# A spiking feed-forward block: the idle row's products move from TensorE to ScalarE and GpSimd, and x comes in 16 loads

## The chip, the core and the metric

The kernel runs on one core of one Trainium2 chip. The core has five engines that run their own instruction streams and meet only at semaphores: TensorE (PE, matrix products; weight loads are shown as PEld), VectorE (DVE), ScalarE (ACT), GpSimd (POOL) and SyncE (SP, which only issues transfers here). Transfers run on 16 DMA engines. The metric is the device time of one execution in microseconds. Before the change it is 115.94 us, the median of three runs (115.93 to 116.21).

## The reference

`x` is (2, 2048, 512). An integrate-and-fire stage turns it into spikes, and a two-layer network is applied to them and added to `x`:

```python
rates = relu(x) * 0.001
c = cond[:, None, :] + cumsum(rates, axis=1)
fl = floor(c)
spikes = (fl - shift(fl)) / 0.001            # mostly 0; a spike is 1000
h = relu(einsum('bsd,dw->bsw', spikes, w1) + b1)      # w1: 512 x 2048
out = x + einsum('bsw,wd->bsd', h, w2) + b2           # w2: 2048 x 512
```

In most tokens no feature spikes. There the network gives the same row for all: the "idle row", `relu(b1) @ w2 + b2`. Over a sequence each of the 2 x 512 features crosses its threshold about once, so at most 1024 of the 4096 rows differ from `x` plus the idle row.

## The kernel before

**What it computes.** Tokens are laid out 16 to a partition: partition p of `x_sb[b]` holds tokens 16p to 16p+15 of sequence b. Five streams of work stand beside each other.

1. *The table* (PE, L718). For a token in which exactly one feature d spikes, the row to be added is a fixed function of d. The kernel computes that row for all 512 features: for each of 16 chunks m of the hidden layer, ScalarE turns the chunk of w1 into `relu(1000*w1 + b1) - relu(b1)` (L380, L381), and PE multiplies it with the chunk of w2 into four PSUM tiles `ps_table` (four products 128x512 in float32 a chunk; the trace shows each as two MATMUL records). The weights of a chunk come as one 512 KB transfer ("pair").
2. *The search* (DVE, with small PE products). `block_totals` adds up relu(x) over the 16 tokens of a partition (L475, L477); `turn_totals` transposes the sums on PE (L749); `block_sums` and `find_blocks` make running sums and find the block in which each feature crosses its threshold; GpSimd gathers those 16 values by indirect DMA (L319, `rates`); `find_tokens` finds the token; PE spreads the tokens (`spread_tokens`, L759), DVE counts which tokens meet others (`count_met`, L537), `find_leads` and `count_leads` number the shared ones, and `find_slots` puts them in 128 slots. All this is done for b = 0 and for b = 1; b = 1 ends later.
3. *The idle row* (PE). `add_strips` multiplies `relu_b1` with w2 in 16 products of 32 output partitions each (L731); ScalarE copies the four strips, `join_strips` adds them with one 128x512 product (L739), ScalarE copies again into `idle_base`, and DVE adds b2 (`finish_idle_row`).
4. *The stores*. `add_idle` (L613) adds the idle row to 4 tokens a partition, 2.2 us for 1 MB; SP stores each of the eight pieces (L280) as soon as it is there. When a sequence's four stores have landed, GpSimd adds table rows into the output by indirect DMA (`add_row`, L324), four scatters for each sequence. These are the single-spike tokens.
5. *The general rows*. For tokens with more spikes, `first_spikes` and `second_spikes` build the spike columns, PE runs both layers (L788, 128 products of 128x128 with ScalarE's relu L399 behind them, then L795, 16 products 128x512), DVE subtracts the idle base (L649) and GpSimd scatters one last time (L324, `to_general`). At the end GpSimd waits for all scatters, loads a flag (`redo_count`, a register load from SBUF) and skips a branch that does not run with these inputs.

**What sets the order.** Each engine's stream is written out by hand. On PE the table's chunks are the filler into which the small products of the search are set at fixed places; an instruction there that has to wait stops all behind it. The same holds for DVE and GpSimd. SP issues the loads in the order in which they are written, alternating a pair and 1 MB of x, and all the loads share the DMA engines.

## Time and profile before

| | |
|---|---|
| median of 3 runs | 115.94 us (115.93 to 116.21) |
| the profiled execution | 116.06 us |
| its span, first to last instruction | 114.2 us |
| PE busy | 97.1 us (85%), 370 instructions |
| DVE busy | 72.2 us (63%) |
| ACT busy | 33.8 us (30%) |
| POOL busy | 27.0 us (24%) |
| DMA | 31.40 MB, mean 275 GB/s |

The profiled execution took 1.86 us more than its span; that part lies outside the instructions. A busy share says how long an engine had work, not that it set the time: an engine can be at 85% and still have room at the place that matters. Views in the section of rows are named by what they show. In a timeline row the columns are start, duration (us), engine, line, operation, output<-input, shape and count, and in brackets the idle time ahead and what ended it.

### The profile page before, as it was taken

The numbers are of one execution on the slowest core, as the hardware profiler recorded it, in microseconds if no ns is written. First come the engines' busy times: TensorE is split into PE (matmuls) and PEld (weight loads), VectorE is DVE, ScalarE is ACT, GpSimd is POOL, SyncE is SP. The second block draws the span as 40 slices with busy tenths as digits, with TensorE's granted clock in tenths as the row PEclk, the third lists the DMA queues.
The fourth block names the chain that finished last, engine by engine and source line by source line (L and its number), as shares of the span: only waits on it lengthen the run. The fifth ranks groups of instructions, "written<-read, shape, count | busy, mean of one in ns | idle before, by whom it ended". The sixth has DMA issues, their size and how long they took to land. (4 is left out here: it accounts for less than half of the span.)

```text
span 114.2 us, 1132 instructions
## 1 busy us (share of the span) xinstructions
PE 97.1 (85%) x370; PEld 51.2 (45%) x370; DVE 72.2 (63%) x161; ACT 33.8 (30%) x59; POOL 27.0 (24%) x32
## 2 busy tenths in 40 slices
PE   0079999999999989999969999999999999996000
PEld 0043444445433444243424754459999944441000
DVE  2004899678999999889778759999999200002000
ACT  3445542354235189930102000006834400000000
POOL 6600000000037400074000000000048740578500
PEclk9999999999999999999999999999999999999975
DMA  1999999999999999999700000699879999477730
GB/s 39 263 368 419 417 429 425 416 417 416 423 413 404 395 390 408 386 384 380 267 13 0 0 0 6 275 413 413 367 324 413 316 327 278 78 77 96 88 47 3
DMA packets 9002, 31.40 MB, mean 275 GB/s; under 512 B 1570, under 2 KB 1698, under 8 KB 7072
## 3 DMA queue, kind: packets, MB, share of 16 engines
q1 hardware_dynamic: 7152, 29.37, 65.5%
q0 software_dynamic: 1552, 1.64, 10.3%
q10 hardware_dynamic: 288, 0.27, 0.9%
q8 instruction: 5, 0.08, 0.4%
q14 instruction: 5, 0.04, 0.1%
HBM read 21.31 MB, written 10.75 MB: 281 GB/s over the span
## 5 line engine op out<-in xcount | busy, mean ns | idle before, releaser
L718 PE MATMUL ps_table<-w_sb 128*128 128x512 f32 x128 | 59.5, 615 | 6.3 <-DMA w_sb<-in_w_pairs 6.3
L718 PEld LDWEIGHTS ps_table<-w_sb 128*128 128x128 f32 x128 | 24.4, 197 | 36.0 <-issue 29.7
L477 DVE SCALAR_TENSOR_TENSOR total<-x_sb,total 128x512 f32<-128x512 f32 x30 | 20.7, 691 | 3.2 <-DMA x_sb<-in_x 2.3
L324 POOL DMA_INDIRECT out<-w_sb,to_single x8 | 13.4, 1674 | 39.2 <-DMA out<-x_sb 37.4
L380 ACT ACTIVATE w_sb<-w_sb,b_col 128x512 f32<-128x512 f32 (+1 forms) x17 | 11.8, 691 | 22.5 <-DMA w_sb<-in_w_pairs 22.5
L319 POOL DMA_INDIRECT rates<-in_x_turned,sixteen_at x8 | 8.4, 1049 | 39.9 <-DVE sixteen_at L503 38.1
L613 DVE TENSOR_TENSOR x_sb<-x_sb,idle_row 128x2048 f32<-128x2048 f32 x8 | 17.8, 2282 | 0.0
L795 PE MATMUL ps_idle<-w_sb 128*128 128x512 f32 x32 | 13.9, 592 | 0.0
L381 ACT ACTIVATE w_sb<-w_sb,minus_relu_b 128x512 f32<-128x512 f32 (+1 forms) x17 | 11.8, 697 | 0.6
L649 DVE TENSOR_TENSOR w_sb<-ps_idle,idle_base 128x512 f32<-128x512 f32 x1 | 0.7, 692 | 15.6 <-PE ps_idle L795 15.6
L795 PEld LDWEIGHTS ps_idle<-w_sb 128*128 128x128 f32 x32 | 6.0, 190 | 7.2 <-issue 7.2
L399 ACT ACTIVATE w_sb<-ps_turn,b_col 128x128 f32<-128x128 f32 x8 | 2.9, 368 | 19.2 <-PE ps_turn L788 19.2
L788 PE MATMUL ps_small<-spk_t,w_sb 128*128 128x128 f32 x64 | 8.5, 275 | 0.0
L788 PE MATMUL ps_turn<-spk_t,w_sb 128*128 128x128 f32 x64 | 8.5, 275 | 0.0
L788 PEld LDWEIGHTS ps_turn<-spk_t,w_sb 128*128 128x128 f32 x64 | 7.9, 192 | 0.5 <-issue 0.5
L788 PEld LDWEIGHTS ps_small<-spk_t,w_sb 128*128 128x128 f32 x64 | 7.8, 192 | 0.0
L475 DVE TENSOR_SCALAR total<-x_sb 128x512 f32<-128x512 f32 x2 | 0.9, 427 | 7.2 <-DMA x_sb<-in_x 7.2
L731 PE MATMUL ps_idle<-w_sb,relu_b 128*32 128x512 f32 x32 | 4.1, 601 | 0.0
L399 ACT ACTIVATE w_sb<-ps_small,b_col 128x128 f32<-128x128 f32 x8 | 2.9, 368 | 3.2 <-PE ps_small L788 3.1
L537 DVE SCALAR_TENSOR_TENSOR same<-ps_turn,token,weigh 128x512 bf16<-128x512 f32 x4 | 3.0, 751 | 0.3 <-DVE hot L556 0.2
L537 DVE SCALAR_TENSOR_TENSOR same<-ps_met,token,weigh 128x512 bf16<-128x512 f32 x4 | 3.0, 750 | 0.1
L749 PEld LDWEIGHTS ps_turn<-ident_dt,total 128*128 128x128 f32 x16 | 1.9, 191 | 2.0 <-DVE total L477 2.0
(111 smaller groups left out, 52.6 us busy)
## 6 DMA issues: line engine op xcount, KB each, us to landing
out<-x_sb SPq DMA_DIRECT2D x8, 1024.0 KB, 4.4
w_sb<-in_w_pairs SPq DMA_DIRECT2D x15, 512.0 KB, 20.1
x_sb<-in_x SPq DMA_DIRECT2D x7, 1024.0 KB, 18.4
w_sb<-in_w SPq DMA_DIRECT2D x4, 1024.0 KB, 18.3
x_sb<-in_x SPq DMA_DIRECT2D x2, 512.0 KB, 6.8
w_sb<-in_w_pairs SPq DMA_DIRECT2D x2, 256.0 KB, 4.1
b_row<-in_b ACTq DMA_DIRECT2D x1, 256.0 KB, 4.3
rates<-in_x_turned,sixteen_at POOLq DMA_INDIRECT x8, 5.4
```

What stands on the lines that cost most here:

```text
L319: pool.indirect_dma_start(out=rates[:, col, :], out_offset=None, in_=x_sixteen, in_offset=bass.IndirectOffsetOnAxis(ap=sixteen_at[:, col:c ...
L324: pool.indirect_dma_start(out=out_rows, out_offset=bass.IndirectOffsetOnAxis(ap=to, axis=0), in_=row, in_offset=None, bounds_check=last_ro ...
L380: chain(act.activation(weights, weights, ACT.Relu, bias=b1_col[:, m:m + 1], scale=PER_DT))
L381: act.activation(weights, weights, ACT.Identity, bias=minus_relu_b1[:, m:m + 1]).then_inc(table_hidden_ready, 1)
L399: act.activation(hidden[m], ps_hidden[m % 2][:, 0:P], ACT.Relu, bias=b1_col[:, m:m + 1], scale=PER_DT).then_inc(ready, 1)
L477: last = dve.scalar_tensor_tensor(out=total[b][:, :], in0=x_sb[b][:, t, :], scalar=0.0, in1=total[b][:, :], op0=ALU.max, op1=ALU.add)
L537: chain(dve.scalar_tensor_tensor(out=same[:, :], in0=ps_spread[b][:, :], scalar=token[:, col:col + 1], in1=weigh[:, (3 - c) * P:(7 - c) * ...
L613: dve.tensor_tensor(tokens, tokens, along(idle_row[:, :], TQ), ALU.add).then_inc(idle_added[b][q], 1)
L718: last = pe.matmul(ps_table[c][:, :], table_hidden[:, m, c * P:(c + 1) * P], w2_sb[:, m, :], start=(m == 0), stop=(m == FC - 1))
L731: last = pe.matmul(ps_idle[strip, :], relu_b1[:, m:m + 1].to_broadcast([P, STRIP]), w2_sb[:, m, :], start=(m < STRIPS), stop=(m >= FC - ST ...
L788: last = pe.matmul(ps_hidden[m % 2][:, 0:P], w1_sb[:, c, m * P:(m + 1) * P], spk_t[:, c, :], start=(c == 0), stop=(c == DC - 1))
L795: last = pe.matmul(ps_out[:, :], hidden[m], w2_sb[:, m, :], start=(m == 0), stop=(m == FC - 1))
```

## The change

Six things are changed together.

- `add_strips` and `join_strips` are gone from PE. ScalarE multiplies each chunk of w2 with `relu_b1` as a per-partition scale (`scale_second`, 16 activations 128x512, into four buffers `scaled`), GpSimd adds the sixteen up (`sum_idle`, 15 additions 128x512, each waiting for the one ahead), and PE sums over the partitions with one product by a matrix of ones (`add_idle_parts`). One of ScalarE's two copies from PSUM goes as well. GpSimd's additions are set around its gathers: 1 to 6 ahead of those of b = 0, 7 to 10 ahead of those of b = 1, and 11 to 15 behind these.
- x comes in 16 loads of 512 KB instead of one pair of half loads and seven of 1 MB; each pair of weights now stands 512 KB earlier in SP's order. `b1_col` and w2's first chunk are issued by ScalarE's queue.
- ScalarE prepares chunk 0 in four pieces and chunk 1 in two.
- PE's small products stand at other places among the table's.
- On DVE `rise_levels` and `names` come first; `find_odd` goes behind `find_leads(0)`; the first `add_idle` goes ahead of `second_spikes`; `list_general` goes behind the last `add_idle`.
- GpSimd loads the redo flag ahead of the last scatter, and waits for the scatters to land at the very end.

```diff
-            for b in range(B):
-                for q in range(XQ):
-                    if b > 0 or q > 0:
-                        load_x(b, q)
-                        load_pair(b * XQ + q + 2)
-            for m in range(B * XQ + 2, FC):
+            load_x(1)
+            load_x(2)
+            for m in range(3, FC):
                 load_pair(m)
+                for h in (2 * m - 3, 2 * m - 2):
+                    if h < B * XH:
+                        load_x(h)
...
+            def sum_idle(begin, end):
+                for m in range(begin, end):
+                    pool.wait_ge(scaled_ready, m + 1)
+                    before = scaled[0] if m == 1 else idle_part
+                    last = pool.tensor_tensor(idle_part[:, :], before[:, :], scaled[m % 4][:, :], ALU.add)
+                    if m < FC - 1:
+                        chain(last)
+                        pool.sem_inc(scaled_used, 1)
+                    else:
+                        last.then_inc(idle_part_ready, 1)
...
+            def scale_second(m):
+                act.wait_ge(w_in[m] if m > 0 else w2_first_in, 16)
+                if m >= 4:
+                    act.wait_ge(scaled_used, max(m - 4, 1))
+                act.activation(scaled[m % 4][:, :], w2_sb[:, m, :], ACT.Copy, scale=relu_b1[:, m:m + 1]).then_inc(
+                    scaled_ready, 1)
...
-            act.wait_ge(strips_summed, 1)
-            act.activation(idle_base[:, :], ps_idle[:, :], ACT.Copy).then_inc(strips_copied, 1)
...
+            def add_idle_parts():
+                pe.wait_ge(idle_part_ready, 1)
+                pe.wait_ge(const_ready, 3)
+                pe.matmul(ps_idle[:, :], ones[:, :], idle_part[:, :], start=True, stop=True).then_inc(idle_summed, 1)
...
+            pool.wait_ge(redo_ready, 1)
+            redo = redo_count(pool)
             pool.wait_ge(general_listed, 1)
             pool.wait_ge(row_ready, 1)
             add_row(to_general[:, :], new_row, general_scattered)
-            pool.wait_ge(singles_scattered, 16 * NE)
-            pool.wait_ge(general_scattered, 16)
...
+            pool.wait_ge(singles_scattered, 16 * NE)
+            pool.wait_ge(general_scattered, 16)
```

The next two listings show PE's stream from `turn_totals(0)` (`ps_turn<-ident_dt,total`) to `spread_tokens(0)` (`ps_met<-ident,token`); `ps_table` are the table's products, `ps_idle` the strips. Before:

```order
L749 MATMUL ps_turn<-ident_dt,total 128x128 x4
L718 MATMUL ps_table<-w_sb 128x512 x9
L731 MATMUL ps_idle<-w_sb,relu_b 32x512 x4
L718 MATMUL ps_table<-w_sb 128x512 x7
L749 MATMUL ps_turn<-ident_dt,total 128x128 x4
L718 MATMUL ps_table<-w_sb 128x512 x5
L731 MATMUL ps_idle<-w_sb,relu_b 32x512 x4
L718 MATMUL ps_table<-w_sb 128x512 x4
L759 MATMUL ps_met<-ident,token 128x128 x4
```

And after (its first row is the 23 table products ahead of the first turn; before there were 19):

```order
L743 MATMUL ps_table<-w_sb 128x512 x23
L763 MATMUL ps_turn<-ident_dt,total 128x128 x4
L743 MATMUL ps_table<-w_sb 128x512 x18
L763 MATMUL ps_turn<-ident_dt,total 128x128 x4
L743 MATMUL ps_table<-w_sb 128x512 x8
L773 MATMUL ps_met<-ident,token 128x128 x4
```

The turn of b = 1 stands behind 41 table products instead of 35, and no strips stand between.

On GpSimd, from the last constant on (`rates` are the gathers, `idle_part` the additions, `to_single` and `to_general` the scatters), it is this after the change:

```order
L307 AFFINE_SELECT weigh<-weigh 128x896
L316 TENSOR_TENSOR idle_part<-scaled 128x512
L316 TENSOR_TENSOR idle_part<-idle_part,scaled 128x512 x5
L328 DMA rates<-in_x_turned,sixteen_at 128x16 x4
L316 TENSOR_TENSOR idle_part<-idle_part,scaled 128x512 x4
L328 DMA rates<-in_x_turned,sixteen_at 128x16 x4
L316 TENSOR_TENSOR idle_part<-idle_part,scaled 128x512 x5
L335 DMA out<-w_sb,to_single 4096x512 x8
L246 TENSOR_LOAD redo_i
L246 ISA x2
L335 DMA out<-w_sb,to_general 4096x512
```

Before, only the eight gathers and the nine scatters stood there, and the TENSOR_LOAD behind the last of them.

On DVE, from the idle row on (`x_sb<-x_sb,idle_row` is `add_idle`, `spk_t<-ps_met,token,spk_t` is `second_spikes`, `single` begins `list_singles`), it is this after the change:

```order
L627 TENSOR_TENSOR idle_row<-b_row,idle_base 128x512
L587 TENSOR_TENSOR spk_t<-token,ps_met 128x512
L573 SCALAR_TENSOR_TENSOR slot<-leads_run,ps_small,leads 128x4
L575 TENSOR_TENSOR hot<-slot,slot_name 128x512
L578 COPY check_sums<-ps_small 128x2
L632 TENSOR_TENSOR x_sb<-x_sb,idle_row 128x2048
L592 SCALAR_TENSOR_TENSOR spk_t<-ps_met,token,spk_t 128x128 x4
L632 TENSOR_TENSOR x_sb<-x_sb,idle_row 128x2048 x3
L581 TENSOR_TENSOR single<-is_first,leads 128x8
L582 TENSOR_SCALAR not_single<-single 128x8
L583 TENSOR_TENSOR to_single<-token,not_single 128x8
L632 TENSOR_TENSOR x_sb<-x_sb,idle_row 128x2048 x4
```

Before, `second_spikes` stood ahead of the first four additions, and eleven more small instructions of `list_general` stood between the two groups of four.

## Rows read from the trace of the kernel before

**Rows 1.** Timeline of GpSimd: gathers, scatters; in brackets idle time and its end.
```profile
3.17 0.28 POOL L305 TENSOR_SCALAR_AFFINE_SELECT upper<-ones 128x128 f32<-128x128 f32 x1
...
48.33 0.95 POOL L319 DMA_INDIRECT rates<-in_x_turned,sixteen_at  x1 [9.63 <-DVE sixteen_at L503]
...
52.10 0.95 POOL L319 DMA_INDIRECT rates<-in_x_turned,sixteen_at  x1 [0.30 <-issue]
84.45 1.90 POOL L324 DMA_INDIRECT out<-w_sb,to_single  x1 [31.39 <-DMA out<-x_sb]
...
98.52 1.55 POOL L324 DMA_INDIRECT out<-w_sb,to_single  x1 [5.98 <-DMA out<-x_sb]
...
104.09 1.55 POOL L324 DMA_INDIRECT out<-w_sb,to_single  x1 [0.30 <-issue]
106.27 1.55 POOL L324 DMA_INDIRECT out<-w_sb,to_general  x1 [0.62 <-issue]
```

**Rows 2.** DMA issues: count, KB each, median us from issue to landing.
```profile
out<-x_sb SPq DMA_DIRECT2D x8, 1024.0 KB, 4.4
...
out<-w_sb,to_general POOLq DMA_INDIRECT x1, 4.8
```

**Rows 3.** Timeline of VectorE, from the second spikes to the end.
```profile
68.28 1.12 DVE L573 SCALAR_TENSOR_TENSOR spk_t<-ps_met,token,spk_t 128x128 f32<-128x128 f32 x4 [1.08 <-PE ps_met L779]
69.32 8.88 DVE L613 TENSOR_TENSOR x_sb<-x_sb,idle_row 128x2048 f32<-128x2048 f32 x4
...
80.36 8.88 DVE L613 TENSOR_TENSOR x_sb<-x_sb,idle_row 128x2048 f32<-128x2048 f32 x4
104.81 0.69 DVE L649 TENSOR_TENSOR w_sb<-ps_idle,idle_base 128x512 f32<-128x512 f32 x1 [15.57 <-PE ps_idle L795]
```

**Rows 4.** Stretches of 2 us: engines' busy time, clock, DMA share, GB/s.
```profile
74.00:76.00 2.00, 2.00 (x6) 0.95 (x5) 2.00 (x2) 0.00 (x0) 0.00 (x0) 1.00 1.02 422
...
82.00:84.00 2.00, 2.00 (x20) 2.00 (x20) 2.00 (x2) 0.91 (x4) 0.00 (x0) 1.00 0.52 217
...
92.00:94.00 2.00, 2.00 (x6) 0.87 (x5) 0.00 (x0) 0.00 (x0) 0.54 (x1) 1.00 1.04 299
```

**Rows 5.** Timeline of TensorE; a table product is two records.
```profile
6.34 18.76 PE L718 MATMUL ps_table<-w_sb 128*128 128x512 f32 x38 [6.34 <-DMA w_sb<-in_w_pairs]
...
26.07 7.89 PE L718 MATMUL ps_table<-w_sb 128*128 128x512 f32 x18
33.90 1.07 PE L731 MATMUL ps_idle<-w_sb,relu_b 128*32 128x512 f32 x8
34.89 6.28 PE L718 MATMUL ps_table<-w_sb 128*128 128x512 f32 x14
41.55 1.16 PE L749 MATMUL ps_turn<-ident_dt,total 128*128 128x128 f32 x8 [0.39 <-DVE total L477]
42.55 4.46 PE L718 MATMUL ps_table<-w_sb 128*128 128x512 f32 x10
...
52.00 1.92 PE L731 MATMUL ps_idle<-w_sb,relu_b 128*32 128x512 f32 x16
...
59.01 0.65 PE L759 MATMUL ps_turn<-ident,token 128*128 128x128 f32 x4 [0.96 <-DVEq L529]
...
76.59 1.05 PE L788 MATMUL ps_turn<-spk_t,w_sb 128*128 128x128 f32 x8
```

**Rows 6.** Timeline of ScalarE, table chunks 0 and 9.
```profile
5.08 0.51 ACT L380 ACTIVATE w_sb<-w_sb,b_col 128x256 f32<-128x256 f32 x1 [1.60 <-DMA w_sb<-in_w_pairs]
...
39.50 0.72 ACT L380 ACTIVATE w_sb<-w_sb,b_col 128x512 f32<-128x512 f32 x1 [3.35 <-DMA w_sb<-in_w_pairs]
```

**Rows 7.** Timeline of VectorE: sums of b = 1 and its search.
```profile
32.82 8.68 DVE L477 SCALAR_TENSOR_TENSOR total<-x_sb,total 128x512 f32<-128x512 f32 x12
...
43.67 1.22 DVE L486 TENSOR_TENSOR_SCAN level<-block_keep,ps_turn 128x512 f32<-128x512 bf16 x1
...
57.41 0.19 DVE L521 TENSOR_SCALAR rates<-rates 128x64 f32<-128x64 f32 x1 [0.82 <-DMA rates<-in_x_turned,sixteen_at]
```

More of the change, by code:

```diff
@@ L71, in spike_ffn @@
         idle_base = sb("idle_base", [P, D])
+        idle_part = sb("idle_part", [P, D])
+        scaled = [sb(f"scaled{i}", [P, D]) for i in range(4)]
         idle_row = sb("idle_row", [P, D])
@@ L387, in _ @@
             act.wait_ge(b1_ready, 2)
-            table_chunk(0, slice(0, 2 * P))
-            table_chunk(0, slice(2 * P, D))
-            for m in range(1, FC):
+            def scale_second(m):
[4 more added lines that the diff above has]
+                    scaled_ready, 1)
+            for c in range(DC):
+                table_chunk(0, slice(c * P, (c + 1) * P))
+            for half in range(2):
+                table_chunk(1, slice(half * 2 * P, (half + 1) * 2 * P))
+            scale_second(0)
+            for m in range(2, FC):
                 table_chunk(m, slice(0, D))
-            act.wait_ge(strips_summed, 1)
-            act.activation(idle_base[:, :], ps_idle[:, :], ACT.Copy).then_inc(strips_copied, 1)
+                scale_second(m - 1)
+            scale_second(FC - 1)
             act.wait_ge(idle_summed, 1)
@@ L640, in _ @@
             find_slots(1)
+            add_idle(0, 0)
             second_spikes()
-            for q in range(XQ):
+            for q in range(1, XQ):
                 add_idle(0, q)
             list_singles()
-            list_general()
             for q in range(XQ):
                 add_idle(1, q)
+            list_general()
             dve.wait_ge(out_summed, 1)
@@ L712, in _, with parts_ready @@
         def _(pe):
+            def parts_ready(m, end):
+                if m == 0:
+                    return end
+                return DC + (end + 1) // 2 if m == 1 else DC + m + 1
             def table_part(m, begin, end):
-                pe.wait_ge(table_hidden_ready, m + 2 if end > 2 or m > 0 else 1)
+                pe.wait_ge(table_hidden_ready, parts_ready(m, end))
                 if m == 0:
@@ L724, in table_chunk @@
                 table_part(m, 0, DC)
-            def add_strips(begin, end):
-                pe.wait_ge(b1_ready, 1)
-                for m in range(begin, end):
-                    pe.wait_ge(w_in[m] if m > 0 else w2_first_in, 16)
-                    strip = slice(m % STRIPS * STRIP, (m % STRIPS + 1) * STRIP)
-                    last = pe.matmul(ps_idle[strip, :], relu_b1[:, m:m + 1].to_broadcast([P, STRIP]), w2_sb[:, m, :],
-                                     start=(m < STRIPS), stop=(m >= FC - STRIPS))
-                if end == FC:
-                    last.then_inc(strips_summed, 1)
-            def join_strips():
-                pe.wait_ge(strips_copied, 1)
-                pe.wait_ge(strip_first_ready, 1)
-                pe.matmul(ps_idle[:, :], strip_first[:, 0:1].to_broadcast([P, P]), idle_base[:, :],
-                          start=True, stop=True).then_inc(idle_summed, 1)
+            def add_idle_parts():
+                pe.wait_ge(idle_part_ready, 1)
+                pe.wait_ge(const_ready, 3)
+                pe.matmul(ps_idle[:, :], ones[:, :], idle_part[:, :], start=True, stop=True).then_inc(idle_summed, 1)
             def turn_totals(b):
```

96 lines of the change are left out of this document (43 added, 53 removed).

## The prediction

> **What bounds the kernel now.** The page gives PE 85% and everything else far less, so the first thing to ask is whether PE sets the end. I read the end of the trace first, then went backwards engine by engine. The last instruction that shows is GpSimd's scatter of the general rows, from 106.27 [rows 1]; it lands 4.8 us later [rows 2], at 111.07, and the span ends at 114.2. Two chains meet in front of it. One is PE's: the second layer ends and DVE's subtraction runs from 104.81 to 105.50 [rows 3]. The other is GpSimd's own: the four scatters of sequence 1 run from 98.52 to 104.09 + 1.55 = 105.64 [rows 1]. They end 0.14 us apart. So a faster PE alone brings nothing; the scatters stand right beside it.
>
> What started the scatters? The row at 98.52 names the landing of the stores. SP stores a piece when DVE has added the idle row; the first addition starts at 69.32, four take 8.88 us (2.22 each), and the second four start at 80.36, 2.16 us behind the end of the first four [rows 3]. While stores run, the DMA engines are full (share 1.02 at 422 GB/s), but in 82 to 84 the share falls to 0.52 [rows 4]: the four stores of sequence 0 are through and the fifth, added at 80.36 to 82.58, is only starting. From 84.45 on GpSimd's scatters share the DMA engines, and the share stays full at 299 GB/s [rows 1, 4]. So the store chain is: first addition, 8 MB through full DMA engines with one hole of about 0.9 us, four scatters, last scatter. The 26.98 us from the first addition's end (71.54) to 98.52 are transfer time, not DVE time.
>
> In front of the first addition stands the search of sequence 1. DVE's sums end at 41.50, `find_bases(0)` fills DVE to 43.67, the running sums start there [rows 7], and from there DVE's chain runs nearly without holes to 67.20 (68.28 less the wait of 1.08 [rows 3]); its one wait on the way is for the gather, 0.82 us at 57.41 [rows 7]. PE serves this chain from between table products.
>
> **The change part by part.**
>
> *PE's strips and join.* The strips cost 0.99 us for four (33.90 to the next start at 34.89) [rows 5], so 16 of them some 3.9 us; the join is a product of the size of the new `add_idle_parts`, so they cancel. PE is 3.9 us shorter. What that buys depends on the two chains above.
>
> *PE's start.* The first transfer has one fewer ahead of it and the first piece is 128 columns instead of 256 (0.51 us each for two activations [rows 6]); I take 0.65 us together, so PE starts at 5.7 instead of 6.34. Each pair comes 512 KB earlier, some 1.25 us at 420 GB/s; chunk 9 before arrives at 39.50 [rows 6] and now near 38. PE wants it at about 39.5 behind ScalarE's 1.4 us: just in time, a wait of 0 to 0.4.
>
> *The turn of sequence 1.* This is the step against the change. PE's first 19 products take at most 18.76 us, a product at speed costs (33.90 - 26.07) / 9 = 0.87, a turn 1.0 (41.55 to 42.55) [rows 5]. After: 5.7 + 18.7 gives 24.4 at most, 4 x 0.87 gives 27.9, the turn 28.9, and 18 x 0.87 gives 44.5; where the first 19 go quicker, since they no longer end in a wait, it is 43.7. I take 44.0. Its result can be read 1.16 later [rows 5], at 45.2, where DVE began at 43.67 [rows 7]. So the search of sequence 1 starts 1.5 us later. The turn of sequence 0 comes at 27.9 instead of 25.08; DVE then is still in the first sums of sequence 1, which the smaller loads of x leave where they are, and it costs nothing.
>
> From 45.2 on everything shifts by 1.5: the gather on GpSimd from 48.33 to 49.8, the wait that ends at 57.41 to 58.9. `find_odd`, moved behind `find_leads(0)`, only fills that wait. DVE reaches the point of 67.20 at 68.7.
>
> *The first addition.* It no longer waits for the slots (1.08 us) nor stands behind the spikes (1.12 us, start to start 1.04) [rows 3]. It begins at 68.7 instead of 69.32 and ends at 70.9 instead of 71.54: 0.6 us earlier. A transfer of 1 MB takes 2.5 us at 422 GB/s [rows 4]; the second addition ends at 70.9 + 1.1 + 2.2 = 74.2, so the DMA engines idle about 0.7 us there, and sequence 0 is through near 82.4, where it was about 82.3. But `list_general` has gone from between the two groups: the fifth addition ends at 74.2 + 4.4 + 0.5 + 2.2 = 81.3 instead of 82.58, and the hole of rows 4 closes. Sequence 1 starts moving at 82.4 instead of about 83.3, and lands 0.9 us earlier, 97.6.
>
> *The end.* Four scatters take 7.12 (98.52 to 105.64) [rows 1], so they end at 104.7. PE meanwhile starts the first layer behind `second_spikes`, at 70.9 + 1.1 = 72.0 instead of 76.59, 4.6 us earlier [rows 5], and DVE's last subtraction ends at 100.9. It is hidden with 3.8 us to spare. The last scatter no longer waits for it and needs 0.3 of idle instead of 0.62 [rows 1]: another 0.3. Loading the flag moves from behind the landing to in front of the scatter. It stands on the same chain in both places, so I count 0; no row shows its duration, but the 3.1 us between landing (111.07) and the end hold it, so it costs between -1 us, if GpSimd does it while the scatter ahead is still being worked on, and 0.5 if it is slower beside them.
>
> *ScalarE.* 16 more activations of 0.72 us [rows 6]. Up to chunk 9 the chunks come 3.8 us apart and three activations need 2.1. Later ScalarE falls to 2.1 us a chunk, and PE needs 3.5. Hidden; chunk 15 is ready about 53, and PE begins it near 64.
>
> *GpSimd's additions.* No row of before shows one. From below: DVE does a two-input 128x512 in 0.69 [rows 3]. The nearest row is GpSimd's own 128x128 select with one input, 0.28 [rows 1], for 512 columns 1.12; with two inputs read one after the other 2.24. I take 1.1 plus 0.06 between two. The Trainium skill ("GPSIMD Engine Reference", section on elementwise cycle accounting) has 4497 ns for 2048 columns, which as an estimate is 1.12 us here; nothing above rests on it. Additions 11 to 15 begin when the gathers end (52.10 + 0.95 + 1.5 = 54.6) and end at 54.6 + 5 x 1.16 = 60.4. PE wants the sum behind the spread of sequence 1, at 59.01 + 0.6 [rows 5] + 1.5 = 61.1. Covered by 0.7 us. Past 1.3 us an addition it would be late by five times the excess.
>
> *Sum.* -0.9 (stores) - 0.3 (last wait) = -1.2 us of the profiled execution's 116.06, 114.86. The median of the runs is 0.12 lower, so I predict 114.7. If the turn comes at 43.7 or 44.5 this is 0.3 less or 0.5 more.
>
> **The rivals.**
>
> *A: GpSimd's additions hold up DVE.* DVE's sums read two tiles (`x_sb`, `total`), as GpSimd's additions do. In before no GpSimd instruction with an input runs beside DVE: the selects are over at 4.7 us and the gathers are the only thing there (DVE's 12 sums beside four of them take 8.68 / 12 = 0.72, their usual price [rows 7]). So nothing in the trace excludes that one waits for the other. Where each addition stops DVE for its 1.16: additions 7 to 9 fall in the sums of sequence 1, which end at 41.50 + 3.5 = 45.0 instead; `find_bases(0)` takes 2.17 and addition 10 falls in it, 48.3. That is 3.1 us behind the 45.2 above, and all that follows shifts: 114.7 + 3.1 = 117.8. It decides from the point where DVE's sums end later than 43.0, since up to there PE's turn at 44.0 and `find_bases(0)` hide it: two additions in full are hardly hidden.
> The Trainium skill says just this ("SBUF - State Buffer", section "Who interferes with whom"): a VectorE instruction with two SBUF inputs and a GpSimd instruction that reads SBUF share a read port, and the second to start waits for the first to finish. No row here shows it. By that rule the time would be the rival's.
>
> *B: the additions are slow.* At 2.3 us each the last five end at 66.1, 5.0 us after PE wants them, and the slots of both sequences stand behind `add_idle_parts` on PE: 119.7. Nothing speaks for it but the missing row.
>
> *C: it cancels.* One addition's worth of delay, or a chunk that PE waits a microsecond for, takes back the 1.2: 115.9. The stores move the same 8 MB through the same full engines, and the margins above are tenths.
>
> *D: PE does count.* If sequence 1 were stored sooner than I think, by the 3.8 us, the end would be PE's, 111. The full DMA share against it makes this 1 in 100.
>
> **How the numbers follow.** The forecast 0.52 (own range 113.6 to 115.5), A 0.26, B 0.07, C 0.14, D 0.01. A measurement tells 0.3%, some 0.35 us, from no change. Faster: the forecast and D and a little of C, 0.54; same 0.13; slower A and B, 0.33. The range goes from the forecast with the flag's load hidden to A's price, 113.5 to 118.0.
>
> **What would show it.** Right: the first `add_idle` near 68.7, the fifth ending near 81.3, no half-empty slice between, the scatters of sequence 1 from 97.6, PE's first layer at 72.0 with its end 4 us ahead of the last scatter. The running sums of sequence 1 on DVE at 45.2, with PE's turn just ahead; where DVE's sums end after 43 and single rows of L496 take over 1 us, it is A; where PE waits for `idle_part`, it is B. Wrong altogether, if the scatters start later than 98.5.

## The result and the profile after

| | before | after |
|---|---|---|
| median of the runs | 115.94 us (115.83 to 116.21) | 118.72 us (117.23 to 119.97) |
| ratio, 95% interval | | 1.012 (1.0084 to 1.0156) |
| profiled execution, its span | 116.06, 114.2 | 117.51, 115.7 |
| forecast, range | | 114.7, 113.5 to 118.0 |

The change makes the kernel slower by 1.2%, some 1.4 us, and by 2.8 us if the two medians of the table are compared. Two of the four executions of after came near 120 us, at granted clocks no lower than those of the others (0.977 and 0.966 against 0.973 and 0.969), and the ratios here and below leave out executions more than 1.5% above the fastest of their kernel, so that for after 117.2 and the profiled 117.5 remain. The forecast was wrong in sign. What came is the mechanism of rival A, GpSimd's additions holding up DVE.

The page's engine shares say at once which way the work went:

```profile
PE 93.0 (80%) x338; PEld 50.5 (44%) x338; DVE 83.4 (72%) x159; ACT 44.4 (38%) x80; POOL 49.6 (43%) x47
```

PE is down as planned. DVE is up, though the change gives it no new work. Its group of the sums over x, in the page's list of the costliest groups, has as many instructions of the same shape as before, where they were 20.7 us at 691 ns each; the second line is what the view of that source line answers in the same trace (ns of the shortest, the median, the longest):

```profile
L496 DVE SCALAR_TENSOR_TENSOR total<-x_sb,total 128x512 f32<-128x512 f32 x30 | 27.7, 923 | 1.0
...
L496 DVE SCALAR_TENSOR_TENSOR total<-x_sb,total x30: 686/693/1919, 11.6 to 43.9; 128x512 f32<-128x512 f32 x30
```

The median is unchanged, and the mean has grown by 232 ns: a few instructions take up to 1919 ns, most of the others their usual 693. A slower engine or tile would lift the median; a long tail under an unchanged median points to somebody in the way. The timelines say who. First DVE's, at the places that answer to [rows 3, 7]:

```profile
33.69 11.81 DVE L496 SCALAR_TENSOR_TENSOR total<-x_sb,total 128x512 f32<-128x512 f32 x12
45.43 1.24 DVE L527 TENSOR_SCALAR some<-blocks_under 128x4 f32<-128x4 f32 x1
...
48.75 1.22 DVE L505 TENSOR_TENSOR_SCAN level<-block_keep,ps_turn 128x512 f32<-128x512 bf16 x1
...
61.10 1.21 DVE L567 TENSOR_TENSOR_SCAN leads_run<-ones,leads 128x4 f32<-128x4 f32 x1
62.55 1.24 DVE L603 TENSOR_SCALAR under_zero<-start_c 128x8 f32<-128x8 f32 x1
64.22 1.03 DVE L540 TENSOR_SCALAR rates<-rates 128x64 f32<-128x64 f32 x1
...
74.88 2.29 DVE L632 TENSOR_TENSOR x_sb<-x_sb,idle_row 128x2048 f32<-128x2048 f32 x1
```

And GpSimd's in the same execution, which answers to [rows 1]:

```profile
40.30 1.28 POOL L316 TENSOR_TENSOR idle_part<-idle_part,scaled 128x512 f32<-128x512 f32 x1
41.77 1.51 POOL L316 TENSOR_TENSOR idle_part<-idle_part,scaled 128x512 f32<-128x512 f32 x1 [0.18 <-POOL idle_part L316]
43.45 1.50 POOL L316 TENSOR_TENSOR idle_part<-idle_part,scaled 128x512 f32<-128x512 f32 x1 [0.18 <-POOL idle_part L316]
45.14 1.50 POOL L316 TENSOR_TENSOR idle_part<-idle_part,scaled 128x512 f32<-128x512 f32 x1 [0.18 <-POOL idle_part L316]
...
61.03 1.26 POOL L316 TENSOR_TENSOR idle_part<-idle_part,scaled 128x512 f32<-128x512 f32 x1 [0.18 <-POOL idle_part L316]
62.47 1.29 POOL L316 TENSOR_TENSOR idle_part<-idle_part,scaled 128x512 f32<-128x512 f32 x1 [0.18 <-POOL idle_part L316]
63.94 1.26 POOL L316 TENSOR_TENSOR idle_part<-idle_part,scaled 128x512 f32<-128x512 f32 x1 [0.18 <-POOL idle_part L316]
...
91.98 3.62 POOL L335 DMA_INDIRECT out<-w_sb,to_single  x1 [26.78 <-DMA out<-x_sb]
...
101.51 1.55 POOL L335 DMA_INDIRECT out<-w_sb,to_single  x1 [0.30 <-issue]
...
108.94 1.55 POOL L335 DMA_INDIRECT out<-w_sb,to_general  x1 [0.30 <-issue]
```

Lay the ends side by side. DVE's `some` ends at 46.67, the addition from 45.14 at 46.64. `leads_run` ends at 62.31 and its addition at 62.29; `under_zero` at 63.79 and its addition at 63.76; `rates` at 65.25 and its addition at 65.20. Four small DVE instructions, 4 to 64 elements wide, which take 0.16 to 0.21 us when nothing runs beside them, each end 0.02 to 0.05 us behind a GpSimd addition. Note that the profile shows this nowhere as a wait: no bracket stands on these DVE rows, since no semaphore is involved. It is hidden in the durations. So the engines do not meet only at semaphores, as the section on the chip puts it.

The account from before to after, by the starts of rows on the way to the end:

| row | before | after | shift | a new part |
|---|---|---|---|---|
| running sums of sequence 1 | 43.67 | 48.75 | +5.08 | +5.08 |
| first `add_idle` | 69.32 | 74.88 | +5.56 | +0.48 |
| fifth scatter | 98.52 | 101.51 | +2.99 | -2.57 |
| last scatter | 106.27 | 108.94 | +2.67 | -0.32 |
| span's end | 114.2 | 115.7 | +1.5 | -1.17 |

So 5.6 us were lost ahead of the first addition of the idle row, and 4.1 were gained behind it. The experiments take both halves apart. Here and below, the running sums are the scan L486 (L505 in after), and the sums are the additions of x ahead of it.

### The profile page after: what moved, and what is told of

Same layout as the page of the kernel before. It is cut to its first block, busy times and chain, and to the rows that moved or that the text cites. A ratio compares the mean times of both kernels' runs of the same rounds, so it can differ in the third digit from the quotient of the medians.

```text
span 115.7 us, 1143 instructions
## 1 busy us (share of the span) xinstructions
PE 93.0 (80%) x338; PEld 50.5 (44%) x338; DVE 83.4 (72%) x159; ACT 44.4 (38%) x80; POOL 49.6 (43%) x47
## 4 chain that ended last, share of the span: by engine, by line
DVE 45%; PE 20%; POOL 10%; issue 9%; DMA 5%; ACT 3%; ACTq 2%; POOLq 0%; DVEq 0%
PE ps_table L743 19%; DVE total L496 10%; POOL out L335 10%; DVE x_sb L632 8%; DMA out<-x_sb 5%; DVE same L556 5%; DVE level L505 2%; DVE under L528 1%; DVE under L519 1%; DVE block_sum L510 1%; DVE hot L575 1%; DVE blocks_under L520 1%; DVE sum_at L531 1%; DVE leads_run L567 1%; DVE some L527 1%
## 5 line engine op out<-in xcount | busy, mean ns | idle before, releaser
L743 PE MATMUL ps_table<-w_sb 128*128 128x512 f32 x128 | 58.8, 612 | 6.0 <-ACT w_sb L395 6.0
L743 PEld LDWEIGHTS ps_table<-w_sb 128*128 128x128 f32 x128 | 24.5, 197 | 34.1 <-issue 26.6
L496 DVE SCALAR_TENSOR_TENSOR total<-x_sb,total 128x512 f32<-128x512 f32 x30 | 27.7, 923 | 1.0
L335 POOL DMA_INDIRECT out<-w_sb,to_single x8 | 14.5, 1815 | 28.9 <-DMA out<-x_sb 26.8
L316 POOL TENSOR_TENSOR idle_part<-idle_part,scaled 128x512 f32<-128x512 f32 x14 | 19.6, 1399 | 13.3 <-ACT scaled L407 12.0
L394 ACT ACTIVATE w_sb<-w_sb,b_col 128x512 f32<-128x512 f32 (+2 forms) x20 | 12.6, 629 | 14.0 <-DMA w_sb<-in_w_pairs 13.9
L407 ACT ACTIVATE scaled<-w_sb,relu_b 128x512 f32<-128x512 f32 x16 | 11.3, 707 | 6.9 <-POOLq L319 6.9
L395 ACT ACTIVATE w_sb<-w_sb,minus_relu_b 128x512 f32<-128x512 f32 (+2 forms) x20 | 12.7, 636 | 0.7
L316 POOL TENSOR_TENSOR idle_part<-scaled 128x512 f32<-128x512 f32 x1 | 1.6, 1621 | 7.8 <-ACT scaled L407 7.8
L420 ACT ACTIVATE idle_base<-ps_idle 128x512 f32<-128x512 f32 x1 | 0.6, 597 | 7.9 <-PE ps_idle L754 7.9
```

What stands on the lines that cost most here:

```text
L316: last = pool.tensor_tensor(idle_part[:, :], before[:, :], scaled[m % 4][:, :], ALU.add)
L335: pool.indirect_dma_start(out=out_rows, out_offset=bass.IndirectOffsetOnAxis(ap=to, axis=0), in_=row, in_offset=None, bounds_check=last_ro ...
L394: chain(act.activation(weights, weights, ACT.Relu, bias=b1_col[:, m:m + 1], scale=PER_DT))
L395: act.activation(weights, weights, ACT.Identity, bias=minus_relu_b1[:, m:m + 1]).then_inc(table_hidden_ready, 1)
L407: act.activation(scaled[m % 4][:, :], w2_sb[:, m, :], ACT.Copy, scale=relu_b1[:, m:m + 1]).then_inc(scaled_ready, 1)
L496: last = dve.scalar_tensor_tensor(out=total[b][:, :], in0=x_sb[b][:, t, :], scalar=0.0, in1=total[b][:, :], op0=ALU.max, op1=ALU.add)
```

## The experiments

Each batch ran beside the kernel before on its own chip, at 116.08, 116.02 and 115.84 us; ratios are to these.

**What the additions cost in all.** `a_noadds` is the changed kernel without additions 1 to 14, so that its idle row lacks most of its terms.

```diff
                     pool.wait_ge(scaled_ready, m + 1)
-                    before = scaled[0] if m == 1 else idle_part
-                    last = pool.tensor_tensor(idle_part[:, :], before[:, :], scaled[m % 4][:, :], ALU.add)
                     if m < FC - 1:
-                        chain(last)
                         pool.sem_inc(scaled_used, 1)
                     else:
-                        last.then_inc(idle_part_ready, 1)
+                        pool.tensor_tensor(idle_part[:, :], scaled[(m - 1) % 4][:, :], scaled[m % 4][:, :],
+                                           ALU.add).then_inc(idle_part_ready, 1)
```

> The changed kernel with GpSimd's additions 1 to 14 left out (waits and counts stay; the idle row is then wrong). Theory 1, the additions hold up VectorE: the 12 sums of sequence 1 take 8.7 us again instead of 11.8, the first add_idle begins near 69 instead of 74.9, and the time falls to about 113.5 to 114.5. Rival, the delay comes from the transposed place of PE's turn or from the smaller loads: the sums still take over 10 us or the first add_idle stays past 72, time over 116.5.

Measured: 111.27 us (111.19 to 111.57), ratio 0.959 (0.955 to 0.963), span 109.4, 2.2 us below the least that I had expected. DVE's timeline:

```profile
33.42 8.68 DVE L494 SCALAR_TENSOR_TENSOR total<-x_sb,total 128x512 f32<-128x512 f32 x12
...
45.58 1.22 DVE L503 TENSOR_TENSOR_SCAN level<-block_keep,ps_turn 128x512 f32<-128x512 bf16 x1 [1.35 <-PE ps_turn L761]
...
68.68 2.29 DVE L630 TENSOR_TENSOR x_sb<-x_sb,idle_row 128x2048 f32<-128x2048 f32 x1
```

The sums are back at 8.68 us. The running sums wait for PE's turn (45.58; the prediction had 45.2), the first addition starts at 68.68 (68.7), and PE's first layer at 72.06 (72.0). Fourteen GpSimd instructions, for whose end nobody stands waiting in after, cost 6.2 us, and without them this kernel is 4.8 us faster than before. GpSimd's timeline of the end:

```profile
85.86 3.54 POOL L333 DMA_INDIRECT out<-w_sb,to_single  x1 [29.59 <-DMA out<-x_sb]
...
95.27 1.54 POOL L333 DMA_INDIRECT out<-w_sb,to_single  x1 [0.30 <-issue]
...
102.66 1.54 POOL L333 DMA_INDIRECT out<-w_sb,to_general  x1 [0.30 <-issue]
```

The fifth scatter stands here at 95.27, where the prediction had 97.6, and it no longer waits for stores. So my account of the end was too dear even without the additions: 2.3 us too late there, and 1.2 behind it.

**Reading or running?** `a_memset` puts three memsets of `idle_part` (512, 512 and 128 columns) in the place of additions 1 to 14: GpSimd is as busy, but only writes.

```diff
...
-                        chain(last)
+                        for cols in (D, D, P):
+                            chain(pool.memset(idle_part[:, 0:cols], 0.0))
...
```

> Each of the 14 additions is replaced by three memsets into idle_part (512, 512 and 128 columns, together about as long as an addition, 1.3 us); they write SBUF and read nothing (the idle row is wrong). Theory 1 in its narrow form, it is the reading of two SBUF tiles by both engines that collides: the sums take 8.7 us, the time is that of the kernel without additions within 0.4 us. Rival 1b, any GpSimd access to SBUF blocks VectorE: the sums take over 11 us and the time is near 117.4. Rival 2, GpSimd's own length is what costs (a late gather, a late scaled buffer): near 117.4 with short sums.

Measured: 112.86 us (112.58 to 114.35), ratio 0.971 (0.966 to 0.976). DVE's sums and, from GpSimd's timeline, memsets beside them:

```profile
33.66 8.68 DVE L496 SCALAR_TENSOR_TENSOR total<-x_sb,total 128x512 f32<-128x512 f32 x12
```

```profile
41.07 1.37 POOL L317 MEMSET idle_part<- 128x512 f32 x3 [0.15 <-POOL idle_part L317]
```

8.68 us beside a GpSimd that is about as busy (47.4 us in all, 49.6 in after): it is what the additions read. The Trainium skill ("SBUF — State Buffer", section "Who interferes with whom") says so for VectorE instructions with two SBUF inputs, and the runs agree, 692 ns a sum beside memsets and 923 beside additions. The 1.6 us over `a_noadds`, where I had expected 0.4 at most, are another thing: the memsets of 11 to 14 keep GpSimd busy until 61.05, and PE waits 1.39 us for the late `idle_part`, rival B in small. One small DVE row beside a memset took 0.56 us instead of 0.16, so a write may not be quite free; that one row doesn't tell.

**The second reader out of SBUF.** `a_psum` is the whole changed kernel, but the sums of x stay in PSUM up to the last token of a block, so that a sum reads one SBUF tile.

```diff
-                        last = dve.scalar_tensor_tensor(out=total[b][:, :], in0=x_sb[b][:, t, :], scalar=0.0,
-                                                        in1=total[b][:, :], op0=ALU.max, op1=ALU.add)
+                        to = run if t < BLK - 1 else total[b]
+                        last = dve.scalar_tensor_tensor(out=to[:, :], in0=x_sb[b][:, t, :], scalar=0.0,
+                                                        in1=run[:, :], op0=ALU.max, op1=ALU.add)
```

> The changed kernel, whole, but the running sums of x lie in PSUM (ps_met, ps_idle) until the 16th token, so that 28 of the 30 two-input sums read only one SBUF tile. Theory 1: the sums no longer wait for GpSimd (about 0.70 to 0.75 us each, 12 in under 9.2 us), totals of sequence 1 are there near 42 instead of 45.4, the first add_idle comes near 71 to 72 (the small operations between 60 and 65 still collide), time 114.5 to 115.5. Rival: the sums are slow for another reason (their input arrives late), time 117 to 118.

Measured: 115.39 us, median of ten that spread from 113.78 to 117.81; ratio 0.988 (0.983 to 0.992); the traced execution took 115.87. DVE's timeline:

```profile
34.59 7.98 DVE L498 SCALAR_TENSOR_TENSOR ps_idle<-x_sb,ps_idle 128x512 f32<-128x512 f32 x11
42.61 0.69 DVE L498 SCALAR_TENSOR_TENSOR total<-x_sb,ps_idle 128x512 f32<-128x512 f32 x1
43.22 0.92 DVE L529 TENSOR_SCALAR some<-blocks_under 128x4 f32<-128x4 f32 x1
...
59.53 1.21 DVE L569 TENSOR_TENSOR_SCAN leads_run<-ones,leads 128x4 f32<-128x4 f32 x1
60.98 1.24 DVE L605 TENSOR_SCALAR under_zero<-start_c 128x8 f32<-128x8 f32 x1
62.65 1.03 DVE L542 TENSOR_SCALAR rates<-rates 128x64 f32<-128x64 f32 x1
```

The sums run at full speed (28 of them at 695 ns in the middle), right beside additions of 1.27 us. But the additions find other victims, and those at 59.5 to 63.7 are the same three as in after. The first addition starts at 73.31, later than the 71 to 72 that I had expected and 1.6 us earlier than in after. Some 2 of the 6.2 us come back, not all.

**The other way round.** `b_dummy` leaves the kernel before as it is and adds 14 GpSimd additions of two tiles that nobody uses, at the same places.

```diff
+            def side_adds(begin, end):
+                for m in range(begin, end):
+                    pool.wait_ge(table_hidden_ready, min(m + 3, FC + 1))
+                    chain(pool.tensor_tensor(side[0][:, :], side[0][:, :], side[1][:, :], ALU.add))
...
+                side_adds(1, 7) if b == 0 else side_adds(7, 11)
...
+            side_adds(11, FC)
```

> The kernel before, whole, with 14 additions 128x512 on GpSimd of two tiles that nothing else reads, at the places where the changed kernel has its own (1 to 6 ahead of the first gathers, 7 to 10 ahead of the second, 11 to 14 behind). Theory 1, the two engines collide over SBUF reads: the sums of sequence 1 take over 11 us instead of 8.7, the first add_idle comes 3 to 5 us later than 69.3, time 119 to 121. Rival, the delay needs something else of the change (PE's order, smaller loads, ScalarE's products): 116 to 116.5. If the first scatter takes 3.5 us instead of 1.9, as in the changed kernel, it is the additions on GpSimd ahead of it that make it slow.

Measured: 128.22 us (126.81 to 129.36), ratio 1.100 (1.092 to 1.108), span 126.3, far above the 119 to 121 that I had expected. Additions alone do it, and here they cost 12.1 us of the span (114.2 before), twice what they cost in the changed kernel. DVE's timeline:

```profile
36.62 11.80 DVE L488 SCALAR_TENSOR_TENSOR total<-x_sb,total 128x512 f32<-128x512 f32 x12
...
116.98 0.69 DVE L660 TENSOR_TENSOR w_sb<-ps_idle,idle_base 128x512 f32<-128x512 f32 x1 [15.56 <-PE ps_idle L806]
```

The same 11.80 us for twelve sums, 3.1 more than in [rows 7]. But before has no slack on PE: its turn stands right behind DVE's sums (41.55 and 41.50 [rows 5, 7]), so that PE loses what DVE loses, and DVE's subtraction behind the second layer starts 12.2 us later than in [rows 3]. In 40 to 60 and in 60 to 80 us PE is busy 17.2 and 16.9 us instead of 18.7 and 20.0, and its mean granted clock is 0.91 in both, where before has 1.00, the level of 2.4 GHz, throughout. PE had waited 2.83 us ahead of its turn at 48.48 and 2.42 us ahead of the product at 69.78, and the clock is 0.60 in 48 to 52 and 0.66 in 68 to 72: part of these stretches is at 1.2 GHz. How the 12.1 us divide between further collisions, waits and clock wasn't taken apart.

**Which additions cost what.** `a_skip_mid` leaves out additions 7 to 10, `a_skip_late` 11 to 14; the edit is one condition (`a_skip_mid`'s is shown), and the idle row lacks these terms.

```diff
                     pool.wait_ge(scaled_ready, m + 1)
+                    if 7 <= m < 11:
+                        pool.sem_inc(scaled_used, 1)
+                        continue
```

> The changed kernel with GpSimd's additions 7 to 10 left out (the idle row is wrong). Theory 1 in parts: these four collide with the 12 sums of sequence 1, so the running sums start at 45.5 instead of 48.75; the additions 11 to 15 still collide with the small operations from 58 to 65, 3 us. First add_idle near 71.7, time 114.2. Rival, the four are harmless because PE's turn hides them: first add_idle still past 74, time near 117.

> The changed kernel with additions 11 to 14 left out (the idle row is wrong). Theory 1 in parts: find_leads, find_odd and find_tokens behind 60 us take their usual 0.2 us an operation, not 1.0 to 1.2; the running sums still start near 48.7, first add_idle near 71.9, time 114.4. Rival, only long VectorE operations suffer: over 116.5.

Measured: `a_skip_mid` 114.85 us (114.47 to 114.98), ratio 0.991 (0.988 to 0.995), first addition at 71.71, as expected, though the time is 0.65 us above the 114.2 expected. `a_skip_late` 116.07, median of ten from 114.22 to 117.58, too unsteady for an interval, first addition at 73.05 where I had expected 71.9. DVE's timeline in `a_skip_mid`:

```profile
34.74 8.67 DVE L499 SCALAR_TENSOR_TENSOR total<-x_sb,total 128x512 f32<-128x512 f32 x12
...
45.58 1.22 DVE L508 TENSOR_TENSOR_SCAN level<-block_keep,ps_turn 128x512 f32<-128x512 bf16 x1
...
59.36 1.24 DVE L606 TENSOR_SCALAR under_zero<-start_c 128x8 f32<-128x8 f32 x1
...
71.71 2.29 DVE L635 TENSOR_TENSOR x_sb<-x_sb,idle_row 128x2048 f32<-128x2048 f32 x1
```

And in `a_skip_late`:

```profile
34.51 12.77 DVE L499 SCALAR_TENSOR_TENSOR total<-x_sb,total 128x512 f32<-128x512 f32 x12
...
49.45 1.22 DVE L508 TENSOR_TENSOR_SCAN level<-block_keep,ps_turn 128x512 f32<-128x512 bf16 x1
...
61.89 0.16 DVE L606 TENSOR_SCALAR under_zero<-start_c 128x8 f32<-128x8 f32 x1
...
73.05 2.29 DVE L635 TENSOR_TENSOR x_sb<-x_sb,idle_row 128x2048 f32<-128x2048 f32 x1
```

The two halves are told apart by the traces of after, `a_skip_mid` and `a_noadds`. Without 7 to 10 the running sums start at 45.58 instead of 48.75 (3.2 us). Without the late ones as well, three small instructions are shorter by 0.8 to 1.1 us each, and the way from the running sums to the first addition takes 23.1 us instead of 26.1. Additions 1 to 6 cost nothing: the running sums start at 45.58 with and without them. Together that is 6.2 us of DVE's time, all of it on the path. `a_skip_late` agrees on the small instructions (`under_zero` 0.16, the way 23.6 us), but its twelve sums took 12.77 us beside the same four additions that made it 11.81 in after, so its first addition comes only 1.8 us earlier. What one collision costs is not the same in every run.

**The gains behind the first addition.** `b_flag` is before with the redo flag loaded ahead of the last scatter, and the landings awaited at the end.

```diff
+            pool.wait_ge(redo_ready, 1)
+            redo = redo_count(pool)
             pool.wait_ge(general_listed, 1)
             pool.wait_ge(row_ready, 1)
             add_row(to_general[:, :], new_row, general_scattered)
-            pool.wait_ge(singles_scattered, 16 * NE)
-            pool.wait_ge(general_scattered, 16)
...
+            pool.wait_ge(singles_scattered, 16 * NE)
+            pool.wait_ge(general_scattered, 16)
```

> The kernel before with only the flag's load moved ahead of the last scatter, and the wait for all scatters moved to the end. Theory: the load is hidden behind the scatter ahead of it, so the stretch from the last scatter's issue to the end shrinks from 7.9 us to 6.8: time 114.8 (1.1 us less). Rival, as predicted: the load costs in front of the scatter what it saved behind it, 115.9, with a gap of over 1 us in front of the last scatter.

Measured: 114.89 us (114.58 to 114.92), ratio 0.989 (0.985 to 0.993), span 113.1. The last scatter in it:

```profile
106.42 1.55 POOL L324 DMA_INDIRECT out<-w_sb,to_general  x1 [0.71 <-DVE w_sb L650]
```

It starts 0.15 us later than in [rows 1], and the span still ends 1.1 earlier. Loading the flag costs a microsecond behind the landing and nothing ahead of the scatter, where it lies in an idle gap.

`b_list` has besides `list_general` behind the last `add_idle`; `b_order` also the first `add_idle` ahead of `second_spikes`:

```diff
             find_slots(1)
+            add_idle(0, 0)
             second_spikes()
-            for q in range(XQ):
+            for q in range(1, XQ):
                 add_idle(0, q)
             list_singles()
-            list_general()
             for q in range(XQ):
                 add_idle(1, q)
+            list_general()
```

> The kernel before with the flag moved and list_general behind the last add_idle, nothing else. Theory 3: the fifth store is issued 1.7 us earlier and is queued behind the fourth; the wait in front of the fifth scatter shrinks from 5.9 us by 3 or more, the first scatter starts a little later; the end is then PE's (104.8): time 114.3 to 114.9, no gain over the flag alone since PE's end stays. Rival: the wait shrinks by 1.7 at most.

> The kernel before with the flag moved, the first add_idle ahead of second_spikes and list_general behind the last add_idle. Theory 3: closing the hole between the stores lets those of sequence 1 get ahead of the scatters; the wait of 6 us in front of the fifth scatter shrinks to under 2, PE's end (about 107, since second_spikes comes 1.1 to 2.2 later and PE is not shorter) becomes the bound: time 114.5 to 115.5. Rival: stores run at the same pace whatever the order, first addition 2 us earlier, scatters 2 us earlier, still over 4 us of wait in front of the fifth: 114.0 to 115.

Measured: `b_list` 114.75 us (114.52 to 115.13), ratio 0.989 (0.986 to 0.992); `b_order` 114.54 (114.43 to 114.61), ratio 0.987 (0.986 to 0.989). The 2-us window with the hole, and GpSimd's rows of the first, the fifth and the last scatter, in `b_list`:

```profile
82.00:84.00 2.00, 2.00 (x20) 2.00 (x20) 2.00 (x2) 0.92 (x3) 0.00 (x0) 1.00 1.00 414
```

```profile
84.37 2.32 POOL L324 DMA_INDIRECT out<-w_sb,to_single  x1 [31.42 <-DMA out<-x_sb]
...
95.70 1.55 POOL L324 DMA_INDIRECT out<-w_sb,to_single  x1 [3.14 <-DMA out<-x_sb]
...
106.16 1.55 POOL L324 DMA_INDIRECT out<-w_sb,to_general  x1 [3.33 <-DVE w_sb L650]
```

The hole of [rows 4] (share 0.52, 217 GB/s) is closed, and the fifth scatter comes 2.9 us earlier than in `b_flag` (98.58), though the first comes only 0.2 earlier. I had valued the hole at its own width, 0.9. The likely reason is in [rows 4] too: once scatters share the DMA engines, the share stays at 1.04 and the rate falls to 299 GB/s, so that each store still waiting then goes slower; stores queued sooner are moved at 414. That link is read from the windows and not tested by itself. Part of the gain is plain: the last addition ends 2.0 us earlier than in `b_flag`, and only the stretch from there to the fifth scatter shrinks by another 0.9 (9.2 to 8.3 us). The wait ahead of the fifth scatter fell by 2.75 us, between the 3 of the theory and the 1.7 of its rival; in `b_order` the fifth scatter starts at 94.05 behind a wait of 2.65, where I had expected under 2. The last scatter doesn't profit in either: it waits for PE, whose chain was the second one in front of the end [rows 3].

**The version without the additions' price.** `a_strips` is the changed kernel with the idle row made by PE's strips and join as before, and PE's places set for it: the turn of sequence 1 behind 39 products instead of 41.

```diff
-            def sum_idle(begin, end):
...
-            def scale_second(m):
...
+            def add_strips(begin, end):
+            def join_strips():
...
-            for m in range(6, 10):
+            for m in range(6, 9):
                 table_chunk(m)
-            table_part(10, 0, 1)
+            table_part(9, 0, 3)
             turn_totals(1)
+            add_strips(0, 8)
```

> The changed kernel with the idle row made by PE's strips and their join as before, ScalarE's products and GpSimd's additions gone, PE's small products put at places to fit (the turn of sequence 1 behind 39 table products). Theory 1: no collision, first add_idle at 67.5 to 69, time 111 to 112.5, limited by PE's end near 103. Rival, the title edit itself is worth its price and the strips cost PE 4 us that show: 114 or more.

Measured: 113.66 us (113.34 to 113.89), ratio 0.979 (0.977 to 0.982), span 111.9. It beats both kernels, though I had expected 111 to 112.5. DVE's timeline:

```profile
33.61 8.67 DVE L478 SCALAR_TENSOR_TENSOR total<-x_sb,total 128x512 f32<-128x512 f32 x12
...
68.03 2.29 DVE L614 TENSOR_TENSOR x_sb<-x_sb,idle_row 128x2048 f32<-128x2048 f32 x1
...
103.89 0.69 DVE L650 TENSOR_TENSOR w_sb<-ps_idle,idle_base 128x512 f32<-128x512 f32 x1 [14.88 <-PE ps_idle L802]
```

Its fifth scatter stands at 95.09, its last at 105.35 behind a wait of 3.13 for that subtraction. Now PE is the bound, and here the strips do count: with them gone and no additions (`a_noadds`) DVE's subtraction starts at 100.39, 3.5 us earlier.

`a_hybrid` tries to have some of it: ScalarE and GpSimd take the first seven products (additions 1 to 6, which are over before the sums of sequence 1), and PE adds the other nine and the sum in ten strips. The cut below is against `a_strips`.

```diff
+            for m in range(1, EARLY):
+                pool.wait_ge(scaled_ready, m + 1)
+                before = scaled[0] if m == 1 else idle_part
+                last = pool.tensor_tensor(idle_part[:, :], before[:, :], scaled[m % 4][:, :], ALU.add)
...
-            add_strips(0, 8)
+            add_strips(0, 6)
...
-            add_strips(8, FC)
+            add_strips(6, 10)
```

> A version meant to be better: of the 16 products of the idle row only the first seven are scaled by ScalarE and added on GpSimd (additions 1 to 6, all before 34 us, while VectorE waits for x anyway); PE makes the other nine as strips and takes GpSimd's sum in as a tenth strip. Theory: no addition falls in the part of VectorE's chain that counts, first add_idle at 68 to 68.7, PE 1.5 us shorter than with 16 strips, time 112.2 (113.7 with all strips on PE). Rival: the six early additions delay the first sums or the gathers, time 113.7 or more.

Measured: 114.68 us (114.41 to 115.06), ratio 0.990 (0.987 to 0.993), 1.0 us above `a_strips`, where I had expected 1.5 below it. DVE's timeline:

```profile
26.61 3.12 DVE L503 SCALAR_TENSOR_TENSOR total<-x_sb,total 128x512 f32<-128x512 f32 x3
...
32.34 1.53 DVE L526 TENSOR_TENSOR under<-block_sum,theta 128x516 f32<-128x516 f32 x1
...
34.91 8.68 DVE L503 SCALAR_TENSOR_TENSOR total<-x_sb,total 128x512 f32<-128x512 f32 x12
```

Three sums take 3.12 instead of 2.1, and a comparison 1.53 instead of 0.7, each beside an addition (27.92, 31.76). The twelve sums start 1.3 us later than in `a_strips`, PE's turn waits 1.18 for them, and DVE's subtraction comes at 104.47. What PE saves on six strips it loses in waits. In `a_hybrid`, then, the early additions are not free either; their other places were not tried.

**The changed kernel once more.** `after_again` ran on the third chip.

> The changed kernel once more, beside the others on the same chip: 117.2 to 117.6, the running sums of sequence 1 at 48.7 and the first add_idle near 75, with a wider spread from run to run than the kernels without additions, since it depends on which of the two engines gets to the memory first.

Measured: 118.07 us (117.14 to 119.53), ratio 1.017 (1.009 to 1.026); sums 33.75 for 11.81, running sums at 48.81, first addition at 74.96, last scatter at 109.02. The positions are those of the first trace within 0.1 us: the collisions are no accident of one execution. The four executions again spread by over 2 us.

## Why the prediction was wrong

What was right, by its own steps:

- *The turn of sequence 1.* 1.5 us later; `a_noadds` shows 1.9. *The first addition* at 68.7 and *PE's first layer* at 72.0: 68.68 and 72.06 there. DVE's last subtraction ends at 101.1 instead of 100.9. The model of DVE's chain stands, without the additions. (PE started at 6.07, not at 5.7.)
- *ScalarE* is hidden: no trace shows a wait of PE for a later chunk that mattered.
- *GpSimd's additions*, that PE would not wait for their sum; but it came so by luck. They take 1.26 to 1.29 us alone and 0.18 between two, against my 1.1 and 0.06. By my own sentence, "Past 1.3 us an addition it would be late by five times the excess", 1.45 with the gap would have been 0.8 us late (an estimate). It stayed hidden only because DVE was later still (the last ends at 65.2, PE's product of the sum starts at 67.14).

What failed is the step *GpSimd's additions*. It asked only how long they take and whether PE would wait for their sum ("Covered by 0.7 us"); it charged DVE nothing and put the charge into rival A at 0.26, for want of a row. The runs showed the charge in two parts. For additions 7 to 10, A was nearly right: a shift of 3.1 us and the running sums at 48.3, where they came 3.2 later than in `a_noadds`, at 48.75. But A counted nothing for additions 11 to 15; they cost 3.0 us on three tiny instructions. Rival A's reason ("sums read two tiles") was too narrow: `under_zero` and `rates` read one tile and were held up as well. The Trainium skill ("SBUF — State Buffer", section "Who interferes with whom") does name `tensor_scalar` among the operations that can take both ports, and these two are of that kind; the trace agrees, with 1.24 and 1.03 us. I had looked only for its sentence on two inputs.

Two more terms were mis-sized, both the other way. *The end*: the flag's load, counted 0 within -1 to 0.5, is worth 1.2 (`b_flag`), just outside my bound. *The first addition*, its last sentences: closing the hole in the stores was -0.9 and is -2.9 at the fifth scatter (`b_list`); from the first addition's start to the fifth scatter after needs 26.6 us (101.51 - 74.88), before 29.2.

Rival A's 117.8 came within 0.3 us of the 117.5 measured, but as a sum of misses: +3.0 for the late additions, -1.2 for the flag, -2.3 for the stores. A total that agrees proves little; the rows on the way (first addition, fifth scatter) do.

Weighing the rule of the Trainium skill named in the prediction against "No row here shows it" was the error of judgement behind the sign. An absent row is no evidence against a rule, and 0.26 treated it as if it were. The ratio of `b_dummy`, 1.10, says what was at stake. And the trace of before wasn't silent. I had written that no GpSimd instruction with an input runs beside DVE, but gathers and scatters read their row numbers from SBUF (`sixteen_at`, `to_single`), and I had looked at DVE's side alone, which lost nothing. GpSimd's side did: the first gather of sequence 0, beside DVE's sums, takes 1.34 us, that of sequence 1 takes 0.95 [rows 1].

```profile
33.20 1.34 POOL L319 DMA_INDIRECT rates<-in_x_turned,sixteen_at  x1 [28.49 <-DVE sixteen_at L503]
```

The scatters tell it more plainly. The first scatter of every run starts while DVE is in an `add_idle`, which reads two SBUF tiles, and it lasts until that addition ends and some 1.5 us more, which is what a scatter takes by itself. DVE's row in after:

```profile
85.22 8.89 DVE L632 TENSOR_TENSOR x_sb<-x_sb,idle_row 128x2048 f32<-128x2048 f32 x4
```

| run | first scatter starts | takes | `add_idle` beside it ends | takes without that wait |
|---|---|---|---|---|
| before | 84.45 | 1.90 | 84.80 | 1.55 |
| `b_list` | 84.37 | 2.32 | 85.17 | 1.52 |
| `b_order` | 82.59 | 2.93 | 84.01 | 1.51 |
| `a_strips` | 83.41 | 3.15 | 85.03 | 1.53 |
| `a_noadds` | 85.86 | 3.54 | 87.90 | 1.50 |
| after | 91.98 | 3.62 | 94.11 | 1.49 |

(An addition is a quarter of its row of four.) In the eight other traces the last column is 1.49 to 1.54. Fourteen traces agree, but none of the runs takes the addition away, so the cause is read and not tested. In after no gap between two scatters is over 0.31 us, so what the first one waits (2.13 us, 0.35 in before) goes on to the end: up to 1.8 us, an estimate, that the gains behind the first addition had to make up for, and that the prediction did not see either.

## What to carry to other kernels

Before work is moved to an idle GpSimd, list what VectorE executes in the same stretch, and charge each overlapping GpSimd instruction that reads SBUF to VectorE's path (here about 1 us for an addition of 1.27), small instructions included, unless VectorE was waiting there anyway; idle time on one engine isn't free capacity if its reads stop another. Find such a loss by comparing the mean and the longest of a group with its median: it appears as longer instructions, never as a wait. When stores and scatters share the DMA engines, a hole in the stores can cost more than its width, probably because what is queued late is moved beside the scatters. And look at how long the first scatter takes: it can be standing behind a VectorE addition.

## What the runs showed of the hardware

- A GpSimd addition 128x512 of two fp32 tiles takes 1.27 us; where it meets VectorE, it can take 1.35 to 1.76. Both sides lose: the 12 sums lose 3.1 us to those beside them.
- VectorE's instructions of 4 to 64 columns take up to 1.24 us instead of 0.16 to 0.21 when they meet one, even with one input in SBUF (`under_zero`, `rates`). Once the second operand of a 128x512 sum is in PSUM, it keeps its 695 ns.
- GpSimd memsets beside VectorE leave its sums at 692 ns.
- A GpSimd scatter of 1.55 us that starts beside a VectorE addition 128x2048 of two SBUF tiles takes 1.8 to 3.6 us, by as much longer as the addition still runs; the VectorE addition keeps its 2.22 us.
- Kernels in which additions 7 to 10 run (after, `a_psum`, `b_dummy`, `a_skip_late`) spread by 2 to 4 us from run to run; the others stay within 0.7, but for `a_memset` with 1.8. The runs don't say why.
